# Selective scan: three of sixteen states a tile multiplied with C on ScalarE, after a turn by TensorE

## The reference

```python
xz = einsum('blc,dc->bld', layernorm(groupnorm(x)), in_proj_w)     # 384 -> 2 x 768
xb, z = split(xz, 2)
xc = silu(causal_conv(xb, conv_w, 4 taps) + conv_b)                # 768 channels
dt, B, C = split(xc @ x_proj_w.T, [24, 16, 16])
dt = softplus(dt @ dt_w.T + dt_b)                                  # 768
h_t[d, n] = exp(dt_t[d] * A[d, n]) * h_(t-1)[d, n] + dt_t[d] * x_t[d] * B_t[n]
y_t[d] = sum_n h_t[d, n] * C_t[n] + xc * D                         # n = 0..15
x1 = x + (y * silu(z)) @ out_proj_w.T
out = x1 + window_attention(groupnorm(x1))                         # layer 2, not touched
```

## Time and profile before

| | us |
|---|---|
| median of three runs | 6706.06 |
| profiled execution | 6707.13 |
| its span, first to last instruction | 6705.0 |
| DVE busy | 6135.1 (92%) |
| TensorE busy | 5904.4 (88%) |
| GpSimd busy | 5335.4 (80%) |
| ScalarE busy | 4675.2 (70%) |

### The profile page before, as it was taken

The page is one execution under the profiler, slowest core; times in us unless marked ns, Lnnn a source line. Parts: engine busy times, 40 slices in busy tenths (PEclk is TensorE's granted clock), DMA queues, the critical chain, the costliest instruction groups (busy, mean ns, idle before and its releaser), DMA issues. The chain is left out here.

```text
span 6705.0 us, 97790 instructions
## 1 busy us (share of the span) xinstructions
PE 5904.4 (88%) x32252; PEld 3656.6 (55%) x32252; DVE 6135.1 (92%) x7735; ACT 4675.2 (70%) x8698; POOL 5335.4 (80%) x4329
## 2 busy tenths in 40 slices
PE   6888888888888888888888888888888869999999
PEld 3555555555555555555555555555555547777776
DVE  6999999999999999999999999999999986666666
ACT  3777777777777777777777777777777753433433
POOL 2999999999999999999999999999999970111100
PEclk8999999999999999999999999999999979999999
DMA  6222222222222222222222222222222212222222
GB/s 263 103 103 103 103 103 103 103 103 103 103 103 103 103 103 103 103 103 103 103 103 103 103 103 103 103 103 103 103 103 103 100 63 69 89 74 88 79 83 71
DMA packets 175200, 681.46 MB, mean 102 GB/s; under 512 B 28044, under 2 KB 28268, under 8 KB 141668
## 3 DMA queue, kind: packets, MB, share of 16 engines
q1 hardware_dynamic: 174692, 675.21, 27.1%
HBM read 502.35 MB, written 153.88 MB: 98 GB/s over the span
## 5 line engine op out<-in xcount | busy, mean ns | idle before, releaser
L938 POOL TENSOR_TENSOR dbx<-u,bb 128x512 f32<-128x512 f32 x3072 | 3819.7, 1274 | 37.7 <-DVE p_da L774 18.6
L774 DVE TENSOR_TENSOR_SCAN p_da<-p_da,state_v,dbx 128x512 f32<-128x512 f32 x2112 | 2621.4, 1274 | 53.0 <-ACT p_da L621 52.9
L621 ACT ACTIVATE p_da<-dt,neg_a 128x512 f32<-128x512 f32 x3072 | 2073.6, 687 | 84.8 <-DVE h L781 9.2
L1072 PEld LDWEIGHTS p_yt<-ident,hc_v 128*128 128x128 f32 x8448 | 1115.4, 152 | 1157.1 <-issue 828.5
L1072 PE MATMUL p_yt<-ident,hc_v 128*128 128x128 f32 x8448 | 1391.9, 295 | 190.3 <-DVE hc_v L790 189.9
L790 DVE TENSOR_TENSOR hc_v<-cc,p_da 128x512 f32<-128x512 f32 x2112 | 1392.0, 666 | 0.0
L947 POOL TENSOR_TENSOR hc_g<-h,cc 128x512 f32<-128x512 f32 x960 | 1221.4, 1272 | 119.8 <-DVE h L781 119.7
L781 DVE TENSOR_TENSOR_SCAN h<-p_da,state_g,dbx 128x512 f32<-128x512 f32 x960 | 1218.4, 1269 | 59.1 <-issue 30.6
L1003 PE MATMUL p_g<-xs,win 128*128 128x512 f32 x2304 | 1171.9, 603 | 73.5 <-ACT zt L573 36.7
L638 ACT ACTIVATE state_v<-p_da 128x1 f32<-128x1 f32 x2112 | 350.9, 166 | 957.2 <-DVE hc_v L790 945.0
L999 PE MATMUL p_g<-xb,cdiag 128*128 128x512 f32 x1536 | 792.6, 624 | 130.6 <-ACT halo L561 130.5
(11 more groups left out here) (155 smaller groups left out, 7288.2 us busy)
## 6 DMA issues: line engine op xcount, KB each, us to landing
bb<-bc_spill SPq DMA_DIRECT2D x128, 1024.0 KB, 10.1
cc<-bc_spill SPq DMA_DIRECT2D x128, 1024.0 KB, 9.9
xc_spill<-xc SPq DMA_DIRECT2D x96, 512.0 KB, 2.6
z_spill<-zt SPq DMA_DIRECT2D x96, 512.0 KB, 3.9
xj<-xc_spill SPq DMA_DIRECT2D x192, 256.0 KB, 4.1
zj<-z_spill SPq DMA_DIRECT2D x192, 256.0 KB, 2.7
cc<-x SPq DMA_DIRECT2D x48, 768.0 KB, 6.0
xc<-in_x SPq DMA_DIRECT2D x33, 768.0 KB, 11.5
```

What stands on the lines that cost most here:

```text
L621: nc.scalar.activation(p_da[n % RD][:], dt[:, d % 2, :], ACT.Exp, scale=neg_a[:, d, n:n + 1])\
L774: nc.vector.tensor_tensor_scan(psum, psum, dbx[:, n % RB, :], state_v[:, d, k:k + 1], ALU.mult, ALU.add).then_inc(s_scan, 1)
L938: nc.gpsimd.tensor_tensor(dbx[:, n % RB, :], u[:, d % 2, :], bb[:, n, :], ALU.mult)\
L1072: last = nc.tensor.matmul(p_yt[d % 2][:, b * P:(b + 1) * P], product[:, b * P:(b + 1) * P], ident[:], start=False, stop=n == NS - 1, is_tr ...
```

## The change

Of the 16 states of a tile, three (4, 7, 11: BY_TURN) get a new path. DVE scans them into h like GpSimd's. TensorE turns h in four pieces into the bank p_yt that is free between softplus and the next tile (`turn_state`, slots 8, 9, 13). There the tokens lie on the partitions, so C is one number a partition, and ScalarE multiplies while it copies to SBUF, four activations with a scale column (`times_ct`, slots 8, 12, 14). TensorE turns these three products back together with yt_s in the next tile (`turn_back`), accumulating. C itself is turned once a chunk (`turn_c`, `copy_ct`). GpSimd has four states for five, DVE nine for eleven. The buffers: hc_v three for five, h seven for five, cc 13 rows for 16. DVE keeps the last column of all seven states of h in one reduce in slot 13. The slots of most side steps change, as do GpSimd's lag (4) and TensorE's lag behind it (6).

```diff
-BY_POOL = (0, 3, 6, 9, 12)
-BY_DVE = tuple(n for n in range(NS) if n not in BY_POOL)
+BY_POOL = (0, 5, 6, 12)
+BY_TURN = (4, 7, 11)
+BY_DVE = tuple(n for n in range(NS) if n not in BY_POOL + BY_TURN)
+BY_H = tuple(sorted(BY_POOL + BY_TURN))
...
-RB, RH, RD = 4, 5, 4
-RV, RG = 5, 3
-LAG, LAG_V, LAG_G = 3, 2, 3
+RB, RH, RD = 4, NHS, 4
+RV, RG = 3, 3
+TURN_STATE_AT, TIMES_CT_AT, KEEP_AT = (8, 9, 13), (8, 12, 14), 13
+LAG, LAG_V, LAG_G = 4, 2, 6
...
-COPY_LATER, SILU_LATER = 2, (4, 2, 3)
+COPY_LATER, SILU_LATER = 0, (9, 6, 3)
...
-COPY_Y_AT, TURN_AT, GATE_AT = 3, 4, 6
+COPY_Y_AT, TURN_AT, GATE_AT = 1, 5, 6
...
+            def times_ct(i, d, n):
+                m, k = i * ND + d, BY_TURN.index(n)
+                act.wait_ge(s_tm, m * NTN + k + 1)
+                if k == 0:
+                    act.wait_ge(s_yb, m + 1 + C_ONE)
+                if d == 0 and k == 0:
+                    act.wait_ge(s_ct, i + 1)
+                for b in range(NT):
+                    last = nc.scalar.activation(hct[:, k, b, :], p_yt[(d + 1) % 2][:, b * P:(b + 1) * P], ACT.Copy,
+                                                scale=ct[:, i % 2, b, n:n + 1])
+                last.then_inc(s_ht, 1)
...
@@ add_skip @@
                 pe.wait_ge(s_dt, m + 1)
+                pe.wait_ge(s_ht, m * NTN + NTN)
...
@@ turn_back @@
+                for k in range(NTN if m else 0):
+                    pe.wait_ge(s_ht, (m - 1) * NTN + k + 1 + NTN)
+                    for b in range(NT):
+                        last = nc.tensor.matmul(p_yt[(d + 1) % 2][:, b * P:(b + 1) * P], hct[:, k, b, :],
+                                                ident[:], start=False, stop=k == NTN - 1, is_transpose=True,
+                                                skip_group_check=True)
...
+            def turn_state(i, d, n):
+
+                m, k = i * ND + d, BY_TURN.index(n)
+                pe.wait_ge(s_scan, m * NS + n + 1 + C_SCAN)
+                if m + 1 < NCH * ND:
+                    pe.wait_ge(s_dt, m + 2)
+                else:
+                    pe.wait_ge(s_gate, m + 1 + C_ONE)
+                pe.wait_ge(s_ht, m * NTN + k + NTN)
+                for b in range(NT):
+                    last = nc.tensor.matmul(p_yt[(d + 1) % 2][:, b * P:(b + 1) * P], h[:, BY_H.index(n), b * P:(b + 1) * P],
+                                            ident[:], start=True, stop=True, is_transpose=True)
+                last.then_inc(s_tm, 1)
```

More of the change, by code:

```diff
@@ L437, in load_c @@
             def load_c(q, k):
-                src = bc_d[q, NS + 4 * k:NS + 4 * k + 4, :].rearrange("(o n) t -> o n t", o=1).to_broadcast([P, 4, CH])
-                sp.dma_start(cc[:, 4 * k:4 * k + 4, :], src).then_inc(s_cl[k], 16)
+                these = [n for n in BY_C if n // 4 == k]
+                at, count = BY_C.index(these[0]), len(these)
+                src = bc_d[q, NS + these[0]:NS + these[0] + count, :].rearrange("(o n) t -> o n t", o=1)
+                sp.dma_start(cc[:, at:at + count, :], src.to_broadcast([P, count, CH])).then_inc(s_cl[k], 16)
             def load_xj(i, d):
@@ L499, in body @@
                             v = i * (ND * NDV) + 5 * NDV + sum(n < 4 * k + 4 for n in BY_DVE) + C_HCV
-                            g = i * (ND * NPL) + 5 * NPL + sum(n < 4 * k + 4 for n in BY_POOL) + RH
+                            g = i * (ND * NPL) + 5 * NPL + sum(n < 4 * k + 4 for n in BY_POOL) + NPL
                             sp.wait_ge(s_hcv, v)
@@ L638, in keep_state, with copy_ct @@
                 nc.scalar.activation(state_v[:, d, k:k + 1], p_da[n % RD][:, CH - 1:CH], ACT.Copy).then_inc(s_stv, 1)
+            def copy_ct(q):
+                act.wait_ge(s_ctm, q + 1)
+                if q > 1:
+                    act.wait_ge(s_ht, (q - 1) * (ND * NTN) + NTN)
+                turned = p_g[1][:, 0:NT * 64].rearrange("p (b c) -> p b c", c=64)
+                nc.scalar.activation(ct[:, q % 2], turned[:, :, 32 + NS:64], ACT.Copy).then_inc(s_ct, 1)
+            def times_ct(i, d, n):
[9 more added lines that the diff above has]
+                last.then_inc(s_ht, 1)
             def affine(part):
@@ L789, in times_c, with keep_states @@
                     dve.wait_ge(s_cl[n // 4], i * 16 + 16)
[L790 removed]
+                nc.vector.tensor_tensor(hc_v[:, (m * NDV + k) % RV, :], cc[:, BY_C.index(n), :], p_da[n % RD][:], ALU.mult)\
                     .then_inc(s_hcv, 1)
[L793 to L798, removed]
+            def keep_states(i, d):
+                dve.wait_ge(s_scan, (i * ND + d) * NS + BY_H[-1] + 1 + C_SCAN)
+                nc.vector.tensor_reduce(state_h[:, d, :], h[:, :, CH - 1:CH], AX.X, ALU.max).then_inc(s_stg, 1)
             def input_stats(c):
@@ L965, in _ @@
             chunks(pool, body)
+            for n in range(NS - LAG, NS):
+                if n in BY_POOL:
+                    times_c(NCH - 1, ND - 1, n)
         @block.tensor
@@ L1082, in turn_back, with turn_c @@
                     last = nc.tensor.matmul(p_yt[(d + 1) % 2][:, b * P:(b + 1) * P], yt_s[:, b * P:(b + 1) * P],
+                                            ident[:], start=b == 0, stop=m == 0, is_transpose=True,
+                                            skip_group_check=True)
[4 more added lines that the diff above has]
+                                                ident[:], start=False, stop=k == NTN - 1, is_transpose=True,
+                                                skip_group_check=True)
+                last.then_inc(s_yb, 1)
+            def turn_c(q):
+                pe.wait_ge(s_xd, q + 1)
+                for b in range(NT):
+                    last = nc.tensor.matmul(p_g[1][:, b * 64:(b + 1) * 64], xd[:, b * P:(b + 1) * P],
+                                            ident[0:64, 0:64], start=True, stop=True, is_transpose=True)
+                last.then_inc(s_ctm, 1)
+            def turn_state(i, d, n):
[6 more added lines that the diff above has]
+                pe.wait_ge(s_ht, m * NTN + k + NTN)
+                for b in range(NT):
+                    last = nc.tensor.matmul(p_yt[(d + 1) % 2][:, b * P:(b + 1) * P], h[:, BY_H.index(n), b * P:(b + 1) * P],
                                             ident[:], start=True, stop=True, is_transpose=True)
-                last.then_inc(s_yb, 1)
+                last.then_inc(s_tm, 1)
             def affine(part):
@@ L1144, in body @@
                             project_x(q, X_AT.index(g))
+                        if g == TURN_C_AT and q < NCH:
+                            turn_c(q)
+                        if n in TURN_STATE_AT:
+                            turn_state(i, d, BY_TURN[TURN_STATE_AT.index(n)])
                         if n >= LAG_V and n - LAG_V in BY_DVE:
```

65 lines of the change are left out of this document (43 added, 22 removed).

## The result

The changed kernel takes 6598.4 us (median of four runs, 6597.98 to 6598.9), the kernel before 6705.8 in the same comparison: a ratio of 0.984, 95% interval 0.9823 to 0.9857. The forecast was 6591 in a range of 6480 to 6740. 107 us were gained, where the sum had 115.

What follows compares the result with a forecast made beforehand. DVE and GpSimd were taken as both full. DVE's 157.1 us plus 2.7 idle plus 3.4 new lateness gives 163.2 us a chunk, 3.6 less than 166.8; times 32, 115 us off 6706.1: 6591 us, range 6480 to 6740.

Steps and rivals of the forecast that it cites:

- Two full engines: Scan layer: DVE and GpSimd both full; relieved from 164.1 to 157.1 and from 162.8 to 155.4 us a chunk.
- One activation, 0.27 us: ScalarE: each new 128-column activation from PSUM with a scale column costs 0.27 us, twelve a tile.
- ScalarE's load: ScalarE rises from 131.3 to 148.9 us a chunk and is slowest engine in tiles d = 2, 3 and 4.
- three heavy stretches: Stretches behind the gates of d = 2, 3 and 4, which hold the Silu blocks; ScalarE 27.6, 27.7, 26.4 us.
- Its price, 3.4 us a chunk: New lateness from ScalarE behind d = 2 to 4: 3.4 us a chunk of its 4.3 us excess over GpSimd.
- DVE's idle of 2.7 stays: DVE's present idle of 2.7 us a chunk, on top of its 157.1 us of work, gives 159.8.
- TensorE: TensorE rises from 145.6 to 153.5 us a chunk; new waits for ScalarE's products priced at 1.0 and 0.8 us.
- the forecast case: Whole kernel: 3.4 us a chunk of new lateness, anything from 1 to 6.5; 6505 to 6690 us, chance 0.47.
- The clean gain: Rival: the four factor buffers cover ScalarE, or an activation costs near 0.19 us; 6482 to 6426 us, chance 0.20.
- no change: Rival: ScalarE and TensorE make the three Silu tiles 28 us each, giving the gain back; 166.9 a chunk, chance 0.10.
- transposes of 0.275 us each: Rival: each transpose occupies TensorE 275 ns, as the skill page has it; 7130 us or more, chance 0.01.
- The slower rival: TensorE and ScalarE hold each other, new waits about 3 us a tile in d = 1 to 3; 6808 us, chance 0.22.

Runs made afterwards that it cites:

- the three runs on the kernel before: The kernel before with two DVE products, one GpSimd product, or all three cut to 8 columns: 6684.0, 6701.1 and 6583.6 us.
- short_heavy: The changed kernel with one of the four activations of each ScalarE product, only in tiles d = 2, 3 and 4: 6495.7 us.
- silu_early: The changed kernel with the first two Silu blocks of the chunk 5 and 4 slots earlier, no work changed: 6858.9 us.
- b_both: The kernel before with two of DVE's products with C and one of GpSimd's cut to 8 columns: 6583.6 us.
- no_back: The changed kernel without eight of the twelve transposes a tile that turn ScalarE's products back, all waits kept: 6598.3 us.
- mean2: The changed kernel with TensorE's mean for the next chunk's layer norm in slot 2 instead of 4: 6552.1 us.
- b_dve: The kernel before with two of DVE's eleven products with C (states 8 and 13) cut to 8 columns: 6684.0 us.
- split: mean2 with the second turned product made by DVE instead of ScalarE in tiles d = 2, 3 and 4: 6579.5 us.

## Why the prediction was right, step by step

**Two full engines.** Right. DVE came to 157.4 us in the chunk read (157.1 in the sum), GpSimd to 155.4 (155.4), and the three runs on the kernel before show that only both together count.

**One activation, 0.27 us.** Measured 0.25 from start to start in the row, 0.284 by busy time. The formula of the Trainium skill, page "ScalarE: Activation LUTs", section "What ACT_TABLE_LOAD costs", gives 0.386 us for the duration and 0.29 for the spacing; the durations here are 0.343 to 0.402, with a median of 0.372. The duration agrees within a tenth; the spacing of 0.25 in the row is a seventh shorter than the formula's.

**ScalarE's load.** Over-sized: 144.9 us a chunk for the 148.9 of the sum, and 25.8, 26.8 and 25.7 in the three heavy stretches for 27.6, 27.7 and 26.4. It is the slowest engine in one of them rather than in three.

**Its price, 3.4 us a chunk.** The place was right, and so is the size by one measure: taking three quarters of the products away in the heavy tiles gives 103 us, 3.2 a chunk. By DVE's waits it is not. The sum laid the 3.4 on top of the 2.7 that ScalarE cost already, 6.1 in all, and ScalarE's p_da came to 3.5, only 0.9 more than before. short_heavy takes away part of the old lateness as well (its 41 us are half of the 81 of the kernel before), and one wait that names TensorE. The reason was half right. The price was argued from the tile's sum of work. silu_early loses 260 us with the same sums, so the sum alone does not decide. How many factors ScalarE has ahead when a Silu block begins fits the six blocks counted above; no run changes that number alone.

**DVE's idle of 2.7 stays.** This gave 159.8 for the base of the sum. The changed kernel reaches 160.1 when ScalarE is relieved. In the order of the kernel before it does not hold: DVE's idle grew with its relief (b_both).

**TensorE.** Its load was put at 153.5 us a chunk and measured 150.5. Taking two of the new groups away gains nothing (no_back), as the forecast case had it. Of the new waits, those for ScalarE's products are 107.2 us before the turned states and 30.1 before the skip term, 0.6 and 0.2 us a tile, for the 1.0 and 0.8 of the sum. What was not seen is the mean: I took the moved slots as free, and MEAN_AT from 2 to 4 cost 46 us, 1.4 a chunk. So the idle time of DVE, 6.5 us in the chunk read for the 6.1 forecast, came out right by luck, through two errors that cancel: less from ScalarE (3.6), more from TensorE (1.4 for the mean, 0.9 for hc_v, 0.7 for the residual), where the sum had nothing. The forecast time of 6591 us owes its closeness to the same luck: mean2, without the slip in the mean, takes 6552.

**The rivals.** The clean gain and no change did not come about. Nor did transposes of 0.275 us each: the twelve new ones start within 1.31 us, 0.109 each, in the kernel after.

```profile
3128.31 1.47 PE L1134 MATMUL p_yt<-ident,hct 128*128 128x128 f32 x12
3129.62 0.60 PE L1118 MATMUL p_yt<-ident,hc_v 128*128 128x128 f32 x4
```

The slower rival, in which TensorE and ScalarE hold each other, is a real mechanism. In this order it costs little: of its signs only the wait for hc_v's buffers shows. In silu_early it appears in full and the kernel takes 6858.9 us. That this is near the 6808 it was given is chance, since the 6808 was worked out for other waits in other tiles.

## What to carry to other kernels

When two engines are full at once, relieve both or expect little: apart the cuts gave 20 and 4 us, together 121. In b_dve the view of waits named a third engine, ScalarE, and not GpSimd. Where an engine is fed through a short ring of buffers by another that has long blocks of side work, count the load tile by tile and ask how full the ring is when the block starts, and what is queued right behind it. Two blocks set back to the slots that had served the kernel before cost 260 us with no work added. When tables of slots are dealt anew, check for each result that someone waits for whether it still comes before its reader: one slot number, 4 for 2, was worth 46 us here, nearly half of what the whole change brought.

## What the runs showed of the hardware that was not expected

- An activation of 64 columns with a scale column costs 0.218 us of ScalarE's time, one of 128 columns 0.284: cutting one in two adds 0.15 us.
- A product cut from 512 to 8 columns still lasted 0.13 to 0.16 us on DVE and 0.20 us on GpSimd. From its start to the next one's it was 0.05 us on DVE and 0.16 on GpSimd (b_both):

```profile
3066.44 0.13 DVE L791 TENSOR_TENSOR hc_v<-cc,p_da 128x8 f32<-128x8 f32 x1
3066.49 2.46 DVE L774 TENSOR_TENSOR_SCAN p_da<-p_da,state_v,dbx 128x512 f32<-128x512 f32 x2
...
3067.53 0.20 POOL L949 TENSOR_TENSOR hc_g<-h,cc 128x8 f32<-128x8 f32 x1
3067.69 2.51 POOL L939 TENSOR_TENSOR dbx<-u,bb 128x512 f32<-128x512 f32 x2
```

- A multiply on DVE that reads 128x512 from PSUM with C broadcast along each 128 columns costs 0.59 us from start to start in split, no more than the plain product (0.59):

```profile
3018.78 0.67 DVE L840 TENSOR_TENSOR hct<-p_yt,ct 128x512 f32<-128x512 f32 x1
3019.37 1.28 DVE L812 TENSOR_TENSOR_SCAN p_da<-p_da,state_v,dbx 128x512 f32<-128x512 f32 x1
```
